# Three edits to a graph and expert kernel: POOL's rests, the order of ScalarE's scores and gate steps, and where the run counts are loaded

## The chip, the cores and the metric

One core of a Trainium2 chip. The metric is the device time of one execution in microseconds; the median of three runs before the change is 4437.22 us.

## The reference, cut to what matters

```python
edge_index = jnp.stack([src, dst])                 # 100000 edges, sorted by dst, 3125 nodes, 256 features
xn = _layernorm(x)
x = x + _L0_gnn_ref(xn, edge_index, ...) + _L0_mix_ref(xn[None], ...)[0]   # GCN, linear attention
x = x + _L0_ffn_ref(_layernorm(x)[None], ...)[0]   # graph attention gates four experts
xn = _layernorm(x)
x = x + _L1_gnn_ref(xn, edge_index, ...) + _L1_mix_ref(xn[None], ...)[0]
x = x + _L1_ffn_ref(_layernorm(x)[None], ...)[0]   # eight dense experts

# _L0_ffn_ref, the gated experts, with the graph attention that makes the gates (16 columns, 4 heads x 4 experts)
h = (x_flat @ W_gat).reshape(M, HEADS, NUM_EXPERTS)
e = leaky_relu((h * att_src).sum(-1)[src] + (h * att_dst).sum(-1)[dst], 0.2)
ee = exp(e - segment_max(e, dst)[dst])
agg = segment_sum(h[src] * (ee / segment_sum(ee, dst)[dst])[:, :, None], dst) + b_gat
scores = _layernorm(agg, ln_gamma, ln_beta).reshape(M, HEADS, NUM_EXPERTS).mean(1)
topk_s, topk_i = top_k(scores, 2); w = softmax(topk_s)
for ei in range(4):
    g = where(topk_i == ei, w, 0.0).sum(-1)
    out = out + g[..., None] * (gelu(x @ W1[ei] + b1[ei]) @ W2[ei] + b2[ei])
```

## The kernel before, in words

The nodes lie as 25 tiles (T) of 125 rows (P). The program is a sequence of blocks; in each block the five engines run their own instruction lists and meet at semaphores. The order on each engine is the order in which the code is written. `alone(eng, signal, value)` is a wait as an instruction of its own.

**The build of the adjacency (lines 436 to 625, about 50 to 632 us).** The counts of edges from each source to each destination are built as a dense matrix by one-hot matmuls. The destinations are split into 125 groups of 25 nodes (5 groups, TG, for each of 25 tiles). The edges are sorted by destination and cut into chunks of 128; a group works through its chunks in runs of four (RUN). There are 276 runs in all, 18 in the first group, two in most groups and one in many of the last. How many runs a group has, and how many came before, is data: `ranges_of` (L475) loads four numbers into an engine's registers.

- DVE makes, for each of a run's four chunks, the one-hot sources (`hot_src`, L519, three of the four) and the one-hot keys (`hot_key`, L522). Each of the four slots has one buffer, so it waits for `hot_used` of PE, one run back.
- ACT makes the fourth source in `make_sources` (L580, L584), one group ahead, and takes a finished group's counts out of PSUM in `take_out` (L593).
- PE loads the group's counts of runs (L475), multiplies two loop-block matmuls (L548, which start the sum) and then, per run and slot, one pair of matmuls (L557, 512 and 113 columns).
- POOL prepares the runs' keys (L496, L499), far ahead.

**The gated experts (lines 1990 to 2622, about 2100 to 2864 us).** PE runs four experts. Each has 5 groups of nodes (G); a group is eight pieces of the first layer (L2456, ACT's Gelu L2564) and five row tiles of the second (L2470, ACT's copy L2578). Experts 0 to 2 write rows to memory (SP, L2400), the last keeps them in `last_rows`.

Beside this the attention gates are made. The edges are in four blocks here (`earlier` is 1). For the first two, PE gathers the source rows by one-hot matmuls. For the last two, POOL gathers them with 256 indirect transfers (`gather_rows`, L2329), and after every second one it rests: two memsets of one column (`rest`, L2339), each awaited. DVE's `sum_up` waits for a block's gathers (`got`), forms the scores and, after ACT's two exponentials in `weigh` (L2548, L2549), the sums. ACT meets the `weigh` of each block at a fixed place of its list: that of the third block in the last group of expert 1, that of the fourth in group 1 of expert 2, after four pieces of that group.

When all sums are stored, POOL gathers them with 25 transfers (L2363). DVE forms the layer norm's variance, ACT its root (L2615), DVE the marks and their distance from the best, ACT the exponential (L2621), DVE the gates; PE turns them (`turn_gates`, L2531) and DVE adds the three stored experts' rows, weighted (L2294), then the last expert's (L2302), and takes the statistics of the next norm (L2307). SP loads the stored rows (L2443) when expert 2's are all stored and the sums are over (`sums_over`). ACT enters expert 3 only after `picks_over`, since `last_rows` holds the fourth block's gathered rows until then.

## Time and profile before

| | us |
|---|---|
| median of three runs (lowest, highest) | 4437.22 (4434.75, 4440.62) |
| profiled execution, its own time | 4442.14 |
| its span | 4440.2 |
| PE busy | 3688.1 (83%) |
| PE weight loads busy | 2662.1 (60%) |
| DVE busy | 2239.0 (50%) |
| ACT busy | 1345.7 (30%) |
| POOL busy | 720.6 (16%) |
| mean granted TensorE clock | 0.905 |

The profile is one execution, taken by the hardware's profiler. Busy time counts an engine's instructions, not its waits, register steps or the issue of transfers. The timeline lists instructions in order of time, merged where equal ones follow each other: start in us, duration in us, engine, line, operation, output<-inputs, count, and in brackets the idle time before it and what ended it ("issue": nothing that the profile shows; "remote": a signal from outside the engine's view). A "q" behind an engine's name is its sequencer.

### The profile page before, as it was taken

Reading aid. Unit: us, or ns where it says so; the run is one execution under the profiler, and the core shown is the slowest. Engines: PE = TensorE matmul, PEld = TensorE weight load, DVE = VectorE, ACT = ScalarE, POOL = GpSimd, SP = SyncE. Lnnn points to the kernel's source line nnn. Section 1 sums busy time; section 2 is a strip of 40 time slices with the busy share of each in tenths; the row PEclk is TensorE's granted clock in tenths of the full one; section 3 lists DMA queues with packets and bytes.
Section 4 is the critical chain, followed back from the end, with each engine's and each line's share of the span. In section 5 each row is a group of like instructions: output and inputs, shape, how many; then the busy total and the mean of one; then the engine's idle time right before and its main releaser. Section 6 shows DMA issues by size and latency. Waiting matters only on the chain. (4 is left out here: it accounts for less than half of the span.)

```text
span 4440.2 us, 92119 instructions
## 1 busy us (share of the span) xinstructions
PE 3688.1 (83%) x23892; PEld 2662.1 (60%) x23943; DVE 2239.0 (50%) x5781; ACT 1345.7 (30%) x2980; POOL 720.6 (16%) x1416
## 2 busy tenths in 40 slices
PE   4888867499969898996889627689798999799998
PEld 2444435366648757964777415479698544467766
DVE  6888877888840021125677330610402867533333
ACT  2555541477740010042111212410000144133333
POOL 3222210000000000001566632000001565000000
PEclk9999985688879989998999858889999999799999
DMA  3111230132234403501221211245154000100000
GB/s 110 44 71 75 84 120 0 57 95 85 66 111 160 151 5 146 202 22 18 76 63 32 40 45 57 91 148 190 62 186 166 1 1 1 21 14 14 7 14 29
DMA packets 124636, 319.63 MB, mean 72 GB/s; under 512 B 42658, under 2 KB 74897, under 8 KB 109228
## 3 DMA queue, kind: packets, MB, share of 16 engines
q1 hardware_dynamic: 111332, 302.42, 19.6%
q0 software_dynamic: 9760, 8.89, 1.4%
q10 hardware_dynamic: 3404, 6.53, 0.4%
q8 instruction: 78, 1.28, 0.1%
q14 instruction: 62, 0.51, 0.0%
HBM read 245.52 MB, written 72.43 MB: 72 GB/s over the span
## 5 line engine op out<-in xcount | busy, mean ns | idle before, releaser
L557 PE MATMUL ps<-hot_key,hot_src 128*126 128x512 bf16 (+1 forms) x2208 | 416.8, 314 | 38.5 <-DVE hot_key L522 21.0
L522 DVE TENSOR_SCALAR hot_key<-col_iota,run_keys 128x625 bf16<-128x625 int16 x1104 | 394.9, 380 | 0.0
L1338 PE MATMUL ps<-gnn_u_thirds,near 125*128 125x256 bf16 x3000 | 337.2, 275 | 23.3 <-issue 23.3
L557 PEld LDWEIGHTS ps<-hot_key,hot_src 128*126 128x126 bf16 x2208 | 212.5, 136 | 234.3 <-DVE hot_key L522 171.6
L1338 PEld LDWEIGHTS ps<-gnn_u_thirds,near 125*128 125x128 bf16 x3000 | 331.0, 141 | 27.8 <-issue 25.0
L2456 PE MATMUL ps<-xnT,ew 128*128 (+2 forms) x640 | 189.2, 449 | 158.3 <-ACT ehT L2564 123.7
L519 DVE TENSOR_SCALAR hot_src<-col_iota,run_srcs 128x125 bf16<-128x125 int16 x828 | 212.3, 256 | 97.0 <-PE ps L557 52.0
L2456 PEld LDWEIGHTS ps<-xnT,ew 128*128 128x128 f32 x640 | 123.1, 199 | 211.6 <-ACT ehT L2564 135.4
L866 PE MATMUL ps<-row_hot,slot_hot 128*128 128x512 f16 x1088 | 221.4, 357 | 2.3 <-DVE row_hot L1079 2.2
L3650 DVE SCALAR_TENSOR_TENSOR xres<-ps,shares,xres 125x256 f32 x200 | 96.8, 484 | 241.6 <-PE ps L3615 220.7
L2470 PE MATMUL ps<-ew,ehT 128*125 128x256 f32 x800 | 203.5, 398 | 0.0
L3604 PE MATMUL ps<-xnT,f 128*128 x640 | 185.4, 437 | 12.1 <-ACTq L3623 4.5
L1079 DVE TENSOR_SCALAR row_hot<-row_iota,row_of 128x670 f16<-128x670 int16 x544 | 190.5, 394 | 0.0
L1338 PE MATMUL ps<-agg_u_thirds,near 125*128 125x257 bf16 x1500 | 175.0, 277 | 10.2 <-issue 9.7
L3604 PE MATMUL ps<-f_h1T,f 128*128 128x313 f32 (+1 forms) x640 | 180.1, 434 | 0.0
L3615 PE MATMUL ps<-fo,f_h2T 128*125 128x256 f32 x800 | 179.2, 379 | 0.0
L1338 PEld LDWEIGHTS ps<-agg_u_thirds,near 125*128 125x128 bf16 x1500 | 169.4, 141 | 16.3 <-issue 15.3
L1338 PE MATMUL ps<-gcn_u_thirds,near 125*128 125x256 bf16 x1500 | 167.4, 275 | 12.5 <-DVEq L1557 12.5
L3631 ACT ACTIVATE f_h1T<-ps,norm_shift,norm_scale 128x313 f32<-128x313 f32 (+1 forms) x160 | 98.0, 612 | 261.5 <-PE ps L3604 261.5
L1620 POOL MEMSET block_mask<- 128x128 f32 x1 | 0.2, 204 | 1090.6 <-POOLq L1537 1090.6
L1338 PEld LDWEIGHTS ps<-gcn_u_thirds,near 125*128 125x128 bf16 x1500 | 165.3, 141 | 14.2 <-issue 12.9
L2500 PE MATMUL ps<-table_thirds,rows_room 125*128 125x144 bf16 x2304 | 154.8, 228 | 14.8 <-issue 9.2
(571 smaller groups left out, 6898.6 us busy)
## 6 DMA issues: line engine op xcount, KB each, us to landing
near<-adjacency SPq DMA_DIRECT2D x80, 1562.5 KB, 6.5
adjacency<-counts SPq DMA_DIRECT2D x125, 312.5 KB, 2.2
own_in<-own_rows SPq DMA_DIRECT2D x34, 512.0 KB, 4.1
expert_rows<-rows_y SPq DMA_DIRECT2D x75, 125.0 KB
rows_room<-expert_rows SPq DMA_DIRECT2D x25, 375.0 KB
pair_in<-high_rows SPq DMA_DIRECT2D x34, 256.0 KB, 4.8
pair_in<-low_rows SPq DMA_DIRECT2D x34, 256.0 KB, 5.7
rows_room<-key_rows SPq DMA_DIRECT2D x8, 1024.0 KB
```

Source lines behind the costliest of these rows:

```text
L519: nc.vector.tensor_scalar(hot_src[:, j, 0:P], col_iota[:, 0:P], run_srcs[:, ds(at, 1), j:j + 1].rearrange("p a j -> p (a j)"), None, ALU.i ...
L522: nc.vector.tensor_scalar(hot_key[:, j, :], col_iota[:], run_keys[:, ds(at, 1), j:j + 1].rearrange("p a j -> p (a j)"), None, ALU.is_equal ...
L557: last = nc.tensor.matmul(sums[:, b:e], hot_src[:, j, :], hot_key[:, j, b:e], start=False, stop=True, skip_group_check=True)
L866: last = nc.tensor.matmul(ps[:, bank, 0:e - b], slot_hot[:, c % RING, :], row_hot[:, c % RING, b:e], start=False, stop=True, skip_group_ch ...
L1079: nc.vector.tensor_scalar(row_hot[:, c % RING, :], row_iota[:], row_of[i][:, c:c + 1], None, ALU.is_equal).then_inc(routes_made, 1)
L1338: last = nc.tensor.matmul(ps[:, j, 0:width], lead_tiles[BUF[j]][:, k, :], parts.thirds[:, k, i, :], start=(k == 0 and i == 0), stop=(k == ...
L2456: last = nc.tensor.matmul(ps[:, piece % 2, 0:n], w1[i][:, c, m * 128:(m + 1) * 128], xnT[:, c, ds(g * NG + first, n)], start=(c == 0), sto ...
L2470: last = nc.tensor.matmul(o, hT[:, c, j * P:(j + 1) * P], w2[i][:, c, :], start=False, stop=(c == 3))
L2500: last = nc.tensor.matmul(pick_bank(piece % 2, k, many)[:, slot * MIDS * HROW:(slot + 1) * MIDS * HROW], src_hot[piece % 2][0:P, tier, edg ...
L3604: last = nc.tensor.matmul(ps[:, piece % 2, 0:n], (w1, w2)[stage][i][:, c, m * 128:(m + 1) * 128], moving, start=(c == 0), stop=(c == 1))
L3615: last = nc.tensor.matmul(o, h2T[:, c, j * P:(j + 1) * P], wo[i][:, c, :], start=(c == 0), stop=(c == 1))
L3631: nc.scalar.activation(hT[:, m, first:first + n], ps[:, piece % 2, 0:n], ACT.Relu, scale=norm_scale[:, stage, ds(e, 1), m], bias=norm_shif ...
```

## The change

It has three parts, and one that goes with the third.

1. POOL: the rest after every second gather is one awaited memset, not two.
2. ACT: the `weigh` of the fourth block stands in group 4 of expert 2, no longer in group 1; the root of the variances and the exponential of the odds stand in group 3 of expert 3, ahead of its rows 0 and 3 (before: in group 2 ahead of row 0, and between groups 2 and 3). On PE `turn_gates` stands in group 4 of expert 3, no longer in group 3.
3. PE in the build: the run counts of the next group are loaded behind the first pair of matmuls of every run, and no longer between two groups; only the first group of a tile still loads ahead of its runs.
4. ACT in the build: `make_sources` returns the count that `take_out` needs, so a group takes one load of the counts, not two.

```diff
@@ the build, PE
                     with pe.Fori(0, T) as tile:
+                        _, runs, before, _ = ranges_of(mybir.EngineType.PE, tile * TG)
                         for k in range(TG):
                             group = tile * TG + k
-                            _, runs, before, _ = ranges_of(mybir.EngineType.PE, group)
...
                                     last.then_inc(hot_used, 1)
+                                    if j == 0 and k < TG - 1:
+                                        _, next_runs, next_before, _ = ranges_of(mybir.EngineType.PE, group + 1)
+                            runs, before = next_runs, next_before
@@ the build, ACT
-                        first, runs, before, upto = ranges_of(mybir.EngineType.Activation, group)
+                        first, runs, before, _ = ranges_of(mybir.EngineType.Activation, group)
...
-                        return upto
+                        return before
...
-                            make_sources(tile * TG + k + 1)
-                            _, _, _, upto = ranges_of(mybir.EngineType.Activation, tile * TG + k)
-                            take_out(tile, k, upto)
+                            take_out(tile, k, make_sources(tile * TG + k + 1))
@@ the gated experts, POOL
                                 if j % 2:
-                                    rest(b * (SLOTS // 2) + (j // 2 - SLOTS))
-
-                        def rest(n):
-
-                            for k in range(2):
-                                nc.gpsimd.memset(idle[:], 0.0).then_inc(rested, 1)
-                                alone(pool, rested, n * 2 + (k + 1))
+                                    nc.gpsimd.memset(idle[:], 0.0).then_inc(rested, 1)
+                                    alone(pool, rested, b * (SLOTS // 2) + (j // 2 + 1 - SLOTS))
@@ the gated experts, PE
-                        expert(3, 1, 0, 3)
-                        expert(3, 1, 3, 4, ahead_of_rows=turn_gates)
-                        expert(3, 1, 4, G)
+                        expert(3, 1, 0, 4)
+                        expert(3, 1, 4, G, ahead_of_rows=turn_gates)
@@ the gated experts, ACT
-                        expert(2, 0, 1)
-                        expert(2, 1, 2, after_piece=weigh_within(earlier * 2 + 1))
-                        expert(2, 2, G)
-
-                        def root_of_variance(rows):
+                        expert(2, 0, 4)
+                        expert(2, 4, G, after_piece=weigh_within(earlier * 2 + 1))
+
+                        def gate_steps(rows):
                             if rows == 0:
                                 act.wait_ge(var_ready, 1)
                                 nc.scalar.activation(gstd, gvar, ACT.Sqrt).then_inc(std_ready, 1)
+                            if rows == 3:
+                                act.wait_ge(marks_ready, 1)
+                                nc.scalar.activation(odds, odds, ACT.Exp).then_inc(odds_ready, 1)
 
                         act.wait_ge(picks_over, 1)
-                        expert(3, 0, 2)
-                        expert(3, 2, 3, after_row=root_of_variance)
-                        act.wait_ge(marks_ready, 1)
-                        nc.scalar.activation(odds, odds, ACT.Exp).then_inc(odds_ready, 1)
-                        expert(3, 3, G)
+                        expert(3, 0, 3)
+                        expert(3, 3, 4, after_row=gate_steps)
+                        expert(3, 4, G)
```

How the instructions move. On PE, in the build's second group of a tile, the difference is this (+ in the changed kernel; L475 is the load of the run counts, L557 the hot matmuls, L551 the end of the loop over runs, L545 and L548 the next group's wait and loop-block matmuls):

```order
 L557 MATMUL ps<-hot_key,hot_src 126x512
 L557 MATMUL ps<-hot_key,hot_src 126x113
+L475 ISA
+L475 TENSOR_LOAD ranges_row
 L553 REGISTER_ALU
 L557 MATMUL ps<-hot_key,hot_src 126x512
...
 L551 REGISTER_ALU
 L551 COMPARE_AND_BRANCH
-L475 ISA
-L475 TENSOR_LOAD ranges_row
 L545 REGISTER_ALU
 L548 ISA
```

The load has gone from the place between the loop's end and the next group into the loop's body, where every run meets it.

On ACT, in expert 2, before (L2564 Gelu of the pieces, L2548 and L2549 the exponentials of `weigh`, L2578 the copies of the rows; the loop that follows is groups 2 to 4, then comes expert 3):

```order
L2559 UNCONDITIONAL_BRANCH
L2564 ACTIVATE ehT<-ps,eb 128x313 x4
L170 ISA
L2548 ACT_TABLE_LOAD
L2548 ACTIVATE rows_room<-rows_room 128x512
L2549 ACTIVATE rows_room<-rows_room 128x512
L2564 ACT_TABLE_LOAD
L2564 ACTIVATE ehT<-ps,eb 128x312 x4
L2578 ACTIVATE rows_y<-ps 125x256 x5
L2559 REGISTER_ALU
L2559 COMPARE_AND_BRANCH
```

and in the changed kernel, ahead of these the loop over groups 0 to 3, behind them that over groups 0 to 2 of expert 3 (L2558 is the Gelu, L2542 and L2543 `weigh`, L2572 the copies):

```order
L2553 UNCONDITIONAL_BRANCH
L2558 ACTIVATE ehT<-ps,eb 128x313 x4
L170 ISA
L2542 ACT_TABLE_LOAD
L2542 ACTIVATE rows_room<-rows_room 128x512
L2543 ACTIVATE rows_room<-rows_room 128x512
L2558 ACT_TABLE_LOAD
L2558 ACTIVATE ehT<-ps,eb 128x312 x4
L2572 ACTIVATE rows_y<-ps 125x256 x5
L2553 REGISTER_ALU
L2553 COMPARE_AND_BRANCH
```

The steps are the same; three whole groups of expert 2 have gone from behind them to ahead of them.

## Rows read from the trace of the kernel before

**Rows 1.** Waits of the gated experts, 2105 to 2860 us: who waited, for whom, us, times, longest

```profile
PE ps L2456 <- ACT ehT L2564: 123.7, 10, 108.2
ACT L2548 <- DVEq L2160: 105.3, 1, 105.3
DVE last_rows L2258 <- ACT last_rows L2615: 88.2, 1, 88.2
...
DVE rows_room L2144 <- DMA last_rows<-node_table,src_idx: 51.3, 1, 51.3
...
ACT rows_y L2578 <- remote: 16.4, 2, 8.2
```

**Rows 2.** Timeline of the build: a two-run group, then two one-run groups

```profile
304.44 3.16 PE L557 MATMUL ps<-hot_key,hot_src 128*126 128x512 bf16 x16
...
305.23 0.26 DVE L519 TENSOR_SCALAR hot_src<-col_iota,run_srcs 128x125 bf16<-128x125 int16 x1 [0.71 <-POOL run_keys L496]
...
308.13 0.48 PE L548 MATMUL ps<-loop_blocks,own_ident 125*126 x2 [0.54 <-issue]
...
308.66 0.70 PE L557 MATMUL ps<-hot_key,hot_src 128*126 128x512 bf16 x3
...
586.20 1.30 PE L557 MATMUL ps<-hot_key,hot_src 128*126 128x512 bf16 x8
...
588.12 1.30 PE L557 MATMUL ps<-hot_key,hot_src 128*126 128x512 bf16 x8
```

**Rows 3.** Waits of DVE in the build, 60 to 632 us

```profile
DVE hot_src L519 <- PE ps L557: 52.0, 74, 1.1
DVE hot_src L519 <- POOL run_keys L496: 35.1, 50, 0.7
```

**Rows 4.** Timeline of POOL: one rest and the next gather

```profile
2136.44 0.12 POOL L2339 MEMSET att_idle<- 128x1 f32 x1
2136.72 0.10 POOL L2339 MEMSET att_idle<- 128x1 f32 x1 [0.15 <-issue]
2137.67 0.99 POOL L2329 DMA_INDIRECT rows_room<-node_table,src_idx  x1 [0.85 <-issue]
```

**Rows 5.** Line 2339: engine, count, ns min/median/max, first and last start

```profile
L2339 POOL MEMSET att_idle<- x256: 98/112/384, 2136.4 to 2617.7; 128x1 f32 x128
```

**Rows 6.** Timeline of ACT in experts 2 and 3: first pieces of groups, and `weigh`

```profile
2501.62 0.52 ACT L2564 ACTIVATE ehT<-ps,eb 128x313 f32<-128x313 f32 x1 [1.78 <-PE ps L2456]
...
2521.83 0.52 ACT L2564 ACTIVATE ehT<-ps,eb 128x313 f32<-128x313 f32 x1 [0.67 <-PE ps L2456]
...
2630.78 1.28 ACT L2548 ACT_TABLE_LOAD   x1 [105.27 <-DVEq L2160]
...
2654.22 0.52 ACT L2564 ACTIVATE ehT<-ps,eb 128x313 f32<-128x313 f32 x1 [0.67 <-PE ps L2456]
...
2739.03 0.52 ACT L2564 ACTIVATE ehT<-ps,eb 128x313 f32<-128x313 f32 x1 [0.67 <-PE ps L2456]
```

**Rows 7.** Line 2363, the gathers of the sums, columns as above

```profile
L2363 POOL DMA_INDIRECT sums_got<-edge_sums,end_i x25: 992/997/1042, 2662.5 to 2693.8; - x25
```

**Rows 8.** Timeline of DVE: last asking, variances, gates, last statistics

```profile
2655.87 0.15 DVE L2060 TENSOR_SCALAR block_f<-block_f 128x1 f32<-128x1 f32 x1
...
2701.74 0.18 DVE L2255 TENSOR_SCALAR last_rows<-last_rows 128x25 f32<-128x25 f32 x1
...
2812.81 0.34 DVE L2287 COPY gates<-ps 125x100 f32<-125x100 f32 x1 [8.33 <-PE ps L2531]
...
2861.79 1.73 DVE L2307 BATCH_NORM_STATS2 norm_stats<-xres 125x6 f32<-125x256 f32 x5
```

**Rows 9.** Timeline of SP: the loads of the stored experts' rows

```profile
2741.57 63.79 SPq L2443 DMA_DIRECT2D rows_room<-expert_rows  x25
```

**Rows 10.** Lines 475 and 551 on PE's sequencer: count, ns min/median/max, first and last start

```profile
L475 PEldq TENSOR_LOAD <-ranges_row x125: 327/334/544, 46.4 to 628.7; - x125
...
L551 PEldq COMPARE_BRANCH  x276: 67/207/239, 61.6 to 630.5; - x138
```

More of the change, by code:

```diff
@@ L600, in _ @@
                         for k in range(TG):
-                            make_sources(tile * TG + k + 1)
-                            _, _, _, upto = ranges_of(mybir.EngineType.Activation, tile * TG + k)
-                            take_out(tile, k, upto)
-                    for k in range(TG):
-                        if k < TG - 1:
-                            make_sources((T - 1) * TG + k + 1)
-                        _, _, _, upto = ranges_of(mybir.EngineType.Activation, (T - 1) * TG + k)
-                        take_out(T - 1, k, upto)
+                            take_out(tile, k, make_sources(tile * TG + k + 1))
+                    for k in range(TG - 1):
+                        take_out(T - 1, k, make_sources((T - 1) * TG + k + 1))
+                    _, _, _, all_runs = ranges_of(mybir.EngineType.Activation, OWNERS - 1)
+                    take_out(T - 1, TG - 1, all_runs)
                     act.wait_ge(deg_ready, 1)
```

## The prediction

> **What bounds the kernel now.** The page gives TensorE (PE) as busy for 83% of the span, but that is an average over stages with different limits, so I read each edit in its own stage. I began with the list of waits of the attention stage (2105 to 2860 us), where two of the three edits lie. Its longest single waits are one event [rows 1]: ScalarE (ACT) sits 105.3 us in front of `weigh` until VectorE (DVE) has the scores of the last block, and PE sits 108.2 us for ACT's Gelu, because that `weigh` stands in the middle of ACT's loop over expert 2. DVE in turn waits 51.3 us for the gathers that POOL issues. So from 2525 us on only POOL's pace counts; behind it stand 3.5 groups of expert 2 and all of expert 3, of which PE could have done a good part in the hole. The 88.2 us that DVE waits at L2258 for ACT's root are the same thing seen later: the variances are ready and ACT has not got there.
>
> The third edit lies in the build of the adjacency (50 to 632 us). There I read the timeline of PE and DVE and the sequencer's records of two lines. One group of 25 nodes with two runs takes 4.22 us from its first hot matmul to the next group's (304.44 to 308.66), with 0.54 us of pure issue before the loop-block matmuls [rows 2]. DVE, which makes the one-hot operands, waits 52.0 + 35.1 = 87.1 us in the stage [rows 3]; these are the only idle microseconds there that a faster PE can win, and about 10 of them belong to the start.
>
> **Edit 1, one memset per rest (POOL).** A pair of gathers with its rest takes 3.5 us. The second memset starts 0.28 us after the first and ends 0.26 us after it; the 0.85 us from the awaited memset to the next gather stand behind whichever is last, so they stay [rows 4]. There are 256 memsets, most near 0.11 us and some up to 0.38 [rows 5]; 128 go, at 0.26 each: 33 us. DVE waits 51.3 us for POOL's last gather [rows 1], more than that, so all of it arrives at the exponentials: their start, R, moves from 2630.8 [rows 6] to 2597.6. Bounds: 0, if the transfers and not the issue limited the gathers, and 38, if the memsets that go were mostly the longer ones. Against 0 speak the 25 gathers of the sums, issued with no rest at 1.3 us each [rows 7], faster than the new pace.
>
> **Edit 2, `weigh` and the gate steps later in ACT's order.** A group of an expert takes 20.2 us (2501.62 to 2521.83) [rows 6]. Now ACT meets `weigh` in group 1 of expert 2, at 2525.5. In the new order the rest of group 1, groups 2 and 3 and half of group 4 run first: 3 x 20.2 = 60.6 more, so ACT and PE arrive at 2586 and wait about 11 us for R = 2597.6. Before, these stood between R and the copy of the gates (R + 182.0 [rows 6, 8]): half a group and 3 groups of expert 2, then groups 0, 1, 2 of expert 3 and the eight pieces of group 3. Now there stand: the other half of group 4 of expert 2 (23.4, as 2630.8 to 2654.2 [rows 6]), a wait of about 2 for `picks_over` (DVE is through with its asking at R + 25.2 [rows 8]), four groups of expert 3 (80.8), the eight pieces of the last one (9 with a table load), some 4 for the tables of the root and the exponential, and 24 that the 25 gathers of the sums cost. That cost is seen before: the three groups left of expert 2 take 84.8 us (2654.22 to 2739.03 [rows 6]) instead of 60.6, and ACT waits twice 8.2 us for signals from elsewhere [rows 1] exactly while POOL issues those gathers (2662.5 to 2693.8 [rows 7]). I leave this price in on both sides. Sum: 23.4 + 2 + 80.8 + 9 + 4 + 24 = 143, against 182: 39 us, of which I keep 38.
>
> What is late next is DVE: its part behind the gates (50.7 us, 2812.81 to 2863.5 [rows 8]) doesn't shrink, and since the gates are now turned one group later, PE gains some 20 us more than arrive. The variances are ready at R + 71 [rows 8] and the root is asked for near R + 119, so the gathers have 48 us to spare. SP's 25 loads of expert rows (63.8 us [rows 9]) no longer wait for expert 2 but for `sums_over`, near R + 32, and end near R + 96, before the gates at R + 143; without that cover their whole length would count. Bounds of this edit: 14, if the dense gathers hurt twice as much beside these loads, and 49, if ACT's waits at the dense gathers shrink by half or so because expert 3 stores nothing.
>
> **Edit 3, the run counts loaded inside the runs.** On PE the load and its address step leave the gap between groups (100 of 125 boundaries; each tile's first group still loads in the open) and go behind the first of a run's four pairs, in every run. The load alone has a median of 334 ns [rows 10], with its register steps 0.55 us. For a two-run group, with S its first hot matmul: the second pair comes at S + 0.67 (0.31 before), the fourth at S + 1.22. The sequencer needs 1.1 us for a run's register steps and its branch (the branch alone 0.21 [rows 10]; an estimate), 1.68 with the load, so the second run starts at S + 1.68. DVE starts on the operands after next when PE has used the first pair, at S + 0.80 as before (305.23), and takes 3.50 for eight, the period less its idle 0.71 [rows 2]. Second run: second pair S + 2.35, fourth S + 2.89, the loop-block matmuls 0.28 later and the next S another 0.53 later, 3.70 against 4.22. Gain 0.52; DVE would be free at S + 4.30 and is started at S + 4.50, so it still isn't the bound. In a one-run group (586.20 to 588.12, 1.92 us [rows 2]) the sequencer had run ahead of the array and the load was covered; now its fourth pair ends later, 2.03, a loss of 0.1. Of the 100 boundaries 82 end a group of two or more runs, 18 one of a single run: 82 x 0.52 - 18 x 0.1 = 41 us. In long groups a run stays at DVE's 1.75 us, half of 3.50, since 1.68 still fits below it. ACT loses one of its two loads per group and is not waited for. Bounds: 77 won (DVE's 87 less the start), and 83 lost, if the 151 additional loads were all exposed (151 x 0.55). I take 41, nearest to the row of the issue gap, 0.54 x 82 = 44.
>
> [...]
>
> **Sum.** 33 + 38 + 41 = 112 us. From the profiled execution's own 4442.1 us (span 4440.2) this gives 4330. That execution is 4.9 above the median of the runs, 4437.2; from the median it is 4325, my forecast.
>
> **Rivals.**
> [...]
> - The load in the run isn't covered. With the longest load on PE, 544 ns [rows 10], the second pair comes at S + 0.88, the second run at S + 1.89, its fourth pair at S + 3.31 and the next S at 4.12: 0.10 x 82 won, 0.3 x 18 lost, together 3 us. 4437 - 71 - 3 = 4363. Against it: the median of 334.
> - Slower: the shorter rest starves the other engines. While the 25 gathers go out without rests, ACT and PE lose 24 us in some 33, 0.73 per us; in the stretch with two memsets a group takes 20.2 us, no more than elsewhere, so two suffice. If one memset did not, the loss would run over the 450 us of resting gathers. The gains and the 11 us of slack before R cover 123 us, so it decides from 0.27 us per us, a third of the dense price; at half the dense price 164 are lost: 4437 - 112 - 11 + 164 = 4478. Against it: the awaited memset and the 0.85 us behind it stay, and they are most of the rest.
> - The edits do nothing, because some other wait is behind each: 4437.
>
> **Chances.** Forecast, with its own spread 4295 to 4345: 0.62. Attention part smaller: 0.15. Load not covered: 0.14. Starvation: 0.06. Nothing: 0.03. A range of 4290 to 4395 takes in the first three cases and most of the bounds. A measurement of this kernel can tell about 0.2%, 9 us, from no change: faster 0.92, within 0.02, slower 0.06.
>
> **What would show it.** In the changed profile: 128 memsets, pair pitch 3.25 us; ACT's wait at `weigh` 5 to 20 us instead of 105, and PE's with it; DVE's wait for the root about 50; from the gates to the end of the norm's statistics still 51; build groups of two runs at 3.7 us with no issue gap before the loop-block matmuls, one-run groups at 2.0, DVE's idle there near 46. Pair pitch at 3.5, two-run groups at 4.1 or more, ACT's wait at `weigh` above 40, or expert groups over 21 us while POOL gathers at rest pace would each prove a step wrong.

## The result, and the profile after

| | before | changed |
|---|---|---|
| median of 4 runs, us | 4438.92 (4434.75 to 4442.48) | 4340.61 (4337.22 to 4343.19) |
| profiled execution, us (span) | 4442.14 (4440.2) | 4337.22 (4335.5) |
| mean granted TensorE clock | 0.905 | 0.914 |

The ratio is 0.9778, with a 95% interval of 0.9766 to 0.9791: the change saves 98.3 us. The forecast was 4325 (4290 to 4395), that is 112 us. Cut by stage, the span shrank by 104.7 us: the build by 23.1 (41 forecast), the stage from the first gather to the end of the norm's statistics by 74 (71 forecast), everything else by 7.6. So the attention stage came as forecast, and the build gave little more than half.

**The attention stage.** The list of waits (2105 to 2770 us; who waited, for whom, us, times, longest), against [rows 1]:

```profile
PE ps L2451 <- ACT ehT L2558: 56.6, 9, 22.9
...
DVE last_rows L2258 <- ACT last_rows L2608: 46.7, 1, 46.7
...
ACT L2542 <- DVEq L2160: 20.0, 1, 20.0
...
ACT last_rows L2572 <- remote: 17.6, 2, 10.9
```

ACT's wait at `weigh` fell from 105.3 to 20.0 us, PE's longest wait for ACT from 108.2 to 22.9, and DVE waits 46.7 us for ACT's root instead of 88.2. The waits for a "remote" signal are still there; they return below.

POOL, one rest and the pair behind it, and the line of the memset (count, ns min/median/max, first and last start), against [rows 4] and [rows 5]:

```profile
2109.01 1.00 POOL L2329 DMA_INDIRECT rows_room<-node_table,src_idx  x1 [0.30 <-issue]
2110.01 0.11 POOL L2334 MEMSET att_idle<- 128x1 f32 x1
2110.98 1.00 POOL L2329 DMA_INDIRECT rows_room<-node_table,src_idx  x1 [0.85 <-issue]
2112.28 1.00 POOL L2329 DMA_INDIRECT rows_room<-node_table,src_idx  x1 [0.30 <-issue]
2113.27 0.12 POOL L2334 MEMSET att_idle<- 128x1 f32 x1
```

```profile
L2334 POOL MEMSET att_idle<- x128: 113/113/318, 2110.0 to 2559.5; 128x1 f32 x128
```

The 0.85 us behind the awaited memset stayed, and the pair takes 2113.27 - 2110.01 = 3.26 us. ACT and DVE, the places of [rows 6] and [rows 8], in their timelines:

```profile
2508.52 0.52 ACT L2558 ACTIVATE ehT<-ps,eb 128x313 f32<-128x313 f32 x1 [0.67 <-issue]
...
2528.74 0.52 ACT L2558 ACTIVATE ehT<-ps,eb 128x313 f32<-128x313 f32 x1 [0.67 <-PE ps L2451]
...
2572.65 1.28 ACT L2542 ACT_TABLE_LOAD   x1 [20.02 <-DVEq L2160]
...
2690.90 1.28 ACT L2608 ACT_TABLE_LOAD   x1
```

```profile
2712.46 0.34 DVE L2287 COPY gates<-ps 125x100 f32<-125x100 f32 x1 [8.47 <-PE ps L2526]
...
2761.43 1.73 DVE L2307 BATCH_NORM_STATS2 norm_stats<-xres 125x6 f32<-125x256 f32 x5
```

The gathers of the sums and SP's loads, the places of [rows 7] and [rows 9]:

```profile
L2358 POOL DMA_INDIRECT sums_got<-edge_sums,end_i x25: 996/1000/1045, 2603.7 to 2635.0; - x25
```

```profile
2602.92 64.42 SPq L2438 DMA_DIRECT2D rows_room<-expert_rows  x25
```

SP's loads are issued by 2667.3, 45 us ahead of the gates. A group still takes 20.2 us (2528.74 - 2508.52) beside the resting gathers. R is 2572.65; the gates are copied 139.8 us later (182.0 before), and from there to the last statistics it is 50.7 us as before.

**The build.** A slow and a fast two-run group on PE, against [rows 2]; DVE's waits from 60 to 609 us and its line 519 in the same window, against [rows 3]; and line 475 on PE's sequencer, against [rows 10]:

```profile
360.94 0.47 PE L548 MATMUL ps<-loop_blocks,own_ident 125*126 x2
361.48 0.47 PE L557 MATMUL ps<-hot_key,hot_src 128*126 128x512 bf16 x2
362.48 2.64 PE L557 MATMUL ps<-hot_key,hot_src 128*126 128x512 bf16 x14 [0.53 <-DVE hot_key L522]
364.99 0.48 PE L548 MATMUL ps<-loop_blocks,own_ident 125*126 x2
365.52 0.47 PE L557 MATMUL ps<-hot_key,hot_src 128*126 128x512 bf16 x2
366.16 1.47 PE L557 MATMUL ps<-hot_key,hot_src 128*126 128x512 bf16 x8 [0.16 <-DVE hot_key L522]
367.81 1.03 PE L557 MATMUL ps<-hot_key,hot_src 128*126 128x512 bf16 x6 [0.18 <-DVE hot_key L522]
368.68 0.46 PE L548 MATMUL ps<-loop_blocks,own_ident 125*126 x2
```

```profile
DVE hot_src L519 <- PE ps L557: 30.2, 62, 1.6
DVE hot_src L519 <- POOL run_srcs L499: 7.3, 7, 1.1
DVE hot_src L519 <- issue: 5.3, 27, 0.2
DVE hot_src L519 <- POOL run_keys L496: 0.7, 1, 0.7
```

```profile
L519 DVE TENSOR_SCALAR hot_src<-col_iota,run_srcs 128x125 bf16<-128x125 int16 x826 | 212.0, 257 | 58.4 <-PE ps L557 30.2 <-POOL run_srcs L499 7.3 <-issue 5.3
```

```profile
L475 PEldq TENSOR_LOAD <-ranges_row x252: 327/333/729, 45.8 to 604.9; - x126
```

The gap of pure issue before the loop-block matmuls is gone. The second group takes 3.69 us (364.99 to 368.68), the forecast 3.70; the first takes 4.05, and the difference stands in front of its second pair, which starts 1.00 us after the first instead of 0.64. The median of PE's loads hardly moved (334 to 333 ns), but 69 of the 252 now take over 400 ns; before, 3 of 125 did. The profile names DVE (hot_key L522) as the releaser of that second pair; what stands in front of it in PE's own queue is the load, from 361.6 to 362.3 as shown further down.

The list of DVE's waits sums to 43.5 us, close to the 46 that the prediction named as a sign, and yet the build fell 18 us short. That list leaves out every wait of 0.15 us or less. With them DVE is idle for 58.4 us ahead of L519 (the figure behind the second bar), 29 less than the 87.4 of the kernel before, where nearly all of the idle time stood in longer waits. The sign looked fulfilled and wasn't.

From PE's records, the groups' periods summed by kind (start of a group's loop-block matmuls to the next group's; a "last" group is the fifth of a tile, with the next load in the open):

```
groups            count   before    after   change   forecast
one run              18     37.1     39.4     +2.3       +1.8
two runs             65    273.2    248.4    -24.8      -33.8
three and more       17    160.5    157.8     -2.7       -8.8
last of a tile       25    110.1    113.0     +2.9        0
```

Split by whether the load in the group's first run took over 400 ns, two-run groups have a median of 3.70 us with a fast load (33 of them) and 3.93 with a slow one (32); one-run groups 2.02 and 2.31; three-run groups 5.57 and 5.83, against 5.96 before. (For one of the 18 one-run groups the trace has no load between its start and the next group's; it is in neither class.) So the question for the experiments was what makes a load slow; beside it, whether the parts add up, and what the rests between gathers really guard.

### The profile page after: what moved, and what is told of

The parts are those of the page before. It is cut to its first block and busy times, and to the rows that moved or that the text cites. A ratio compares the mean times of both kernels' runs of the same rounds, so it can differ in the third digit from the quotient of the medians.

```text
span 4335.5 us, 91902 instructions
## 1 busy us (share of the span) xinstructions
PE 3669.1 (85%) x23942; PEld 2659.2 (61%) x23943; DVE 2243.8 (52%) x5781; ACT 1344.7 (31%) x2979; POOL 699.8 (16%) x1288
## 5 line engine op out<-in xcount | busy, mean ns | idle before, releaser
L557 PE MATMUL ps<-hot_key,hot_src 128*126 128x512 bf16 (+1 forms) x2208 | 414.5, 314 | 75.5 <-DVE hot_key L522 48.1
L522 DVE TENSOR_SCALAR hot_key<-col_iota,run_keys 128x625 bf16<-128x625 int16 x1104 | 394.6, 379 | 0.0
L557 PEld LDWEIGHTS ps<-hot_key,hot_src 128*126 128x126 bf16 x2208 | 216.0, 137 | 264.6 <-DVE hot_key L522 182.9
L519 DVE TENSOR_SCALAR hot_src<-col_iota,run_srcs 128x125 bf16<-128x125 int16 x828 | 212.5, 257 | 68.4 <-PE ps L557 30.2
L3609 PEld LDWEIGHTS ps<-fo,f_h2T 128*125 128x125 f32 x800 | 150.2, 188 | 26.2
```

The lines of the kernel that those rows point to most:

```text
L519: nc.vector.tensor_scalar(hot_src[:, j, 0:P], col_iota[:, 0:P], run_srcs[:, ds(at, 1), j:j + 1].rearrange("p a j -> p (a j)"), None, ALU.i ...
L522: nc.vector.tensor_scalar(hot_key[:, j, :], col_iota[:], run_keys[:, ds(at, 1), j:j + 1].rearrange("p a j -> p (a j)"), None, ALU.is_equal ...
L557: last = nc.tensor.matmul(sums[:, b:e], hot_src[:, j, :], hot_key[:, j, b:e], start=False, stop=True, skip_group_check=True)
L3609: last = nc.tensor.matmul(o, h2T[:, c, j * P:(j + 1) * P], wo[i][:, c, :], start=(c == 0), stop=(c == 1))
```

## The experiments

In the expectations S is the start of a group's loop-block matmuls, 0.54 us ahead of the first hot matmul, which is the prediction's S. Twelve kernels ran in three sets of four, each set on one chip beside the kernel before: 4437.7 us on the first, 4416.6 on the second, 4439.6 on the third. Differences below are to the kernel before, or the changed kernel, of the same set; in the second set, where the changed kernel didn't run, ratios are compared.

### First set: the edits apart

`e1`: the kernel before with one memset per rest (the POOL hunk of the diff alone). 

> The kernel before with edit 1 alone (one memset per rest; ACT's order and the build as before). Theory: only POOL's pace counts before R, so the exponentials of the last block start 32 us earlier in the stage and everything behind them keeps its length (R to the copy of the gates 182 us): 4437 - 32 = 4405, pair pitch 3.27 us. Rival: the gain of edit 1 needs edit 2, because ACT's late order gives part of it back behind R: under 20 us, 4420 or more.

`e2`: the kernel before with the two hunks on `expert(...)` and `gate_steps` alone. 

> The kernel before with edit 2 alone (weigh in group 4 of expert 2, gate steps in group 3 of expert 3, gates turned in group 4). In the changed kernel ACT still waited 20 us at weigh; with the old rests R is 32 us later against ACT's arrival, so the wait is 52 us, and R to the copy of the gates is 140 us instead of 182: 4437 - 42 = 4395. Rival: the shorter stretch behind R came partly from edit 1 (transfers of the last block out of the way); then R to gates stays above 150 and the kernel above 4405.

Measured: `e1` 4406.85 us (ratio 0.9935, 0.992 to 0.995), -30.8; `e2` 4397.61 (0.9915, 0.990 to 0.993), -40.1. ACT's wait at `weigh` in each (timeline of `e1`, then of `e2`):

```profile
2599.56 1.28 ACT L2544 ACT_TABLE_LOAD   x1 [72.37 <-DVEq L2160]
```

```profile
2628.39 1.28 ACT L2547 ACT_TABLE_LOAD   x1 [39.99 <-DVEq L2160]
```

The first theory holds for both edits, each works without the other: R to the gates is 177.3 us in `e1` (2599.56 to 2776.87; 182 forecast) and 141.0 in `e2` (2628.39 to 2769.40; 140 forecast). The wait in `e2` was forecast at 52 and is 40: ACT came to `weigh` 12 us later than I had worked out from the changed kernel (at 2588.4, close to the 2586 of the prediction), which cost nothing, since R waits for POOL.

`e3`: the kernel before with both halves of edit 3. 

> The kernel before with edit 3 alone (the run counts loaded inside the runs on PE, ACT one load per group less). The build ended 23 us earlier in the changed kernel, and the three edits lie in stages apart: 4437 - 23 = 4414, build groups of two runs 3.7 to 3.8 us. Rival: the edits interact by the DMA or by where the code lies, and the sum of the three alone differs from 98 us by more than 10.

`e3pe`: PE's half only. 

> As the last one, but only PE's half of edit 3: ACT keeps its two loads per group (250 instead of 126). Theory A, register loads of different engines delay one another: in the changed kernel 69 of PE's 252 loads took over 400 ns, so with twice as many loads on ACT some 80 to 110 do, and the gain falls to 15 to 20 us (4417 to 4422). Theory B, PE's loads in a run are slow for a reason of PE's own and ACT is never waited for: as many slow loads and the same time as with both halves, 4414.

Measured: `e3` 4412.7 us (0.9939, 0.9925 to 0.9952), -25.0; `e3pe` 4405.7 (0.9932, 0.9919 to 0.9946), -32.0; these two can't be told apart. The three edits alone sum to 30.8 + 40.1 + 25.0 = 95.9, together they gave 98.3: they add up. The loads of `e3pe`:

```profile
L475 PEldq TENSOR_LOAD <-ranges_row x252: 327/332/627, 45.6 to 599.2; - x126
L475 ACTq TENSOR_LOAD <-ranges_row x250: 303/307/632, 49.7 to 603.2; - x125
```

Both theories fell. With twice as many loads on ACT, not more but fewer of PE's were slow: 20 of 252, against 70 in `e3`. PE's instructions are the same in both, so neither the number of loads on ACT nor PE's own code decides. What moved is ACT's take-out of a group, and with it the moment at which SP issues the group's store. I therefore set every register load of PE, ACT and POOL against the time since SP's last issue of a store (`adjacency <- counts`). All loads that started 0.7 to 1.2 us behind it were slow (over 400 ns), in the kernel before, the changed one, `e3` and `e3pe` alike: 10 of 10, 43 of 43, 40 of 40, 20 of 20. In the pair of groups above SP issued at 360.84 and at 365.10:

```profile
360.84 0.33 SPq L618 DMA_DIRECT2D adjacency<-counts  x1
```

```profile
365.10 0.33 SPq L618 DMA_DIRECT2D adjacency<-counts  x1
```

```profile
L475 POOLq TENSOR_LOAD <-ranges_row x1: 555/555/555, 361.5 to 361.5; - x1
...
L475 PEldq TENSOR_LOAD <-ranges_row x1: 687/687/687, 361.6 to 361.6; - x1
```

```profile
L475 POOLq TENSOR_LOAD <-ranges_row x1: 317/317/317, 365.3 to 365.3; - x1
...
L475 PEldq TENSOR_LOAD <-ranges_row x1: 342/342/342, 365.7 to 365.7; - x1
```

(The last two fences are line 475 in 0.3 us of each group.) The loads 0.64 and 0.76 us behind the issue take 555 and 687 ns, those 0.16 and 0.56 us behind it 317 and 342.

`e3pe` shows a second thing. With 50 fewer slow loads its 65 two-run groups are together no shorter than those of `e3` (248.2 and 247.9 us). The 17 of them that open a tile take 3.95 us (median), against 3.74 in `e3`: behind each of the 17 the loop-block matmuls start 0.14 us after the end of ACT's take-out, which the trace names as their releaser, and in `e3` they don't wait for it. So ACT "is not waited for" holds only with ACT's second load gone, and part 4 of the change is needed, by some 17 x 0.21 = 3.6 us (an estimate from these medians).

### Second set: moving the load, moving the store, and the gathers of the sums

`j2`, in the build on PE:

```
-                                    if j == 0 and k < TG - 1:
+                                    if j == 2 and k < TG - 1:
```

> The changed kernel with PE's load of the run counts behind a run's third pair instead of its first. In the runs so far every register load that starts 0.75 to 1.25 us after SP issued a group's store took 450 to 730 ns, on PE, ACT and POOL alike, and nearly none outside; PE's first-run loads start at S + 0.67, inside that window. Theory A, SP's store delays register loads: behind the third pair the load starts at about S + 1.2, past the window, so under 20 of 252 loads take over 400 ns (69 before), groups of two runs come to 3.7 us, and the kernel gains 5 to 12 us on the changed one (4340.6): 4329 to 4336. Theory B, the load is slow in a group's first run because PE meets that code there first: 60 to 70 loads stay slow, and the time stays within 3 us of 4341.

Measured: 4334.4 us, ratio 0.9819 (0.9805 to 0.9833), against 0.9778 and 0.9788 for the two measurements of the changed kernel: worse by some 15 us, although only 37 loads were slow. The build ended at 619.8 us, that of `space` (below), which has the changed kernel's build and ran on the same chip, at 605.2. That the time lies in theory A's range of 4329 to 4336 is luck: the range was worked out from another chip, on which the kernel before took 21 us more. Theory A's count missed too (37 slow loads, under 20 forecast); it is right on what makes a load slow and wrong on what that is worth. DVE's waits in its build say why:

```profile
DVE hot_src L519 <- PE ps L557: 73.8, 145, 1.3
```

In the changed kernel the load sits behind pair 1, and the pairs behind it follow closely. Behind pair 3 it delays the fourth pair of each run, the last of the group too: by the medians over the 65 two-run groups the last two pairs start at S + 2.85 and 3.54 and the next group at 3.99; in the changed kernel, at 3.19, 3.47 and 3.77. The place behind the first pair is the better of the two tried.

`splate`, on SP:

```
                             alone(sp, group_out, tile * TG + (k + TG + 1))
+                            for _ in range(24):
+                                sp.sem_inc(waits_met, 1)
```

> The changed kernel with SP issuing each group's store about 1 us later (24 semaphore increments between its wait and the store; nothing else is moved). Theory A, SP's store delays register loads: PE's first-run loads now start before the store does and are fast, and those loads that happen to lie 0.75 to 1.25 us behind the new issue are slow instead, whoever makes them; of PE's 252 under 35 take over 400 ns. Theory B, PE's own code is the cause: the same 69 loads stay slow. The time moves by under 10 us either way, since the store is waited for by nobody for four groups.

Measured: 4316.2 us, ratio 0.9774 (0.9758 to 0.9789), no different from the changed kernel's 0.9778; the build ended at 601.6, 3.6 us before that of `space`. The store went out some 1.4 us later, and of the 124 loads in a group's first run 5 were slow instead of 68. But 65 of 252 were slow all the same: now those of the second run, and more of ACT's (37) and POOL's (26). The number forecast (under 35) missed; that the slow loads follow the store is shown, since nothing but SP's issue was moved. Here 79 of 79 loads in the window were slow.

`space`, on POOL, and `spgate`, which has `space` and this order besides:

```
                                                     bounds_check=LIST2 - 1, oob_is_err=False).then_inc(ends_got, 16)
+                            if d % 2:
+                                nc.gpsimd.memset(idle[:], 0.0).then_inc(rested, 1)
+                                alone(pool, rested, earlier * SLOTS + (d // 2 + 1))
```

```
-                        expert(3, 1, 0, 4)
-                        expert(3, 1, 4, G, ahead_of_rows=turn_gates)
+                        expert(3, 1, 0, 3)
+                        expert(3, 1, 3, 4, ahead_of_rows=turn_gates)
+                        expert(3, 1, 4, G)
...
-                        expert(3, 0, 3)
-                        expert(3, 3, 4, after_row=gate_steps)
-                        expert(3, 4, G)
+                        expert(3, 0, 2)
+                        expert(3, 2, 3, after_row=gate_steps)
+                        expert(3, 3, G)
```

> The changed kernel with the same rest (one awaited memset per pair) also between the 25 gathers of the sums. Theory A, POOL's dense issue of gathers holds up signals of the other engines: ACT's two long waits for signals from elsewhere (10.9 us the longest) go, the groups of experts 2 and 3 beside those gathers take 20.2 us instead of 26.5 and 42.8, R to the copy of the gates shrinks from 140 to about 118, and the kernel gains 20 to 23 us: 4318 to 4321. The gathers end 8 us later, which nobody waits for. Theory B, the cost comes from what the gathers and SP's loads of rows move through the DMA engines, whatever their spacing: the waits stay, and the time is 4341.

> The last kernel, and the gate steps and the turning of the gates one group earlier (group 2 and group 3 of expert 3), since ACT waited 20 us at weigh, where 11 were forecast. If the gathers' spacing gives its 22 us, the root is asked for near R + 76, 3 us ahead of the variances (R + 79), the gates are copied near R + 100, DVE's 51 us behind them stay, and ACT's last rows are there before DVE comes to them: another 15 to 20 us, 4299 to 4305. Rival: DVE or the gates' inputs are late (ACT waits over 10 us for the variances, or DVE for SP's rows, which land up to R + 92), and the gain over the last kernel is under 8 us.

Measured: `space` 4314.6 us, ratio 0.9779 (0.9764 to 0.9795), so no gain over the changed kernel's ratio; `spgate` 4295.8, 0.9726 (0.971 to 0.9741), 18.8 us below `space` (15 to 20 forecast). The trace of `space` has the 119 us from R to the gates that theory A wanted, but so have `j2` and `splate`, whose gathers of the sums are as dense as ever. ACT's waits in `j2` beside them (2623 to 2660 us), all short and none remote:

```profile
ACT last_rows L2572 <- PE ps L2465: 19.6, 10, 2.7
ACT ehT L2558 <- PE ps L2451: 7.0, 13, 0.6
```

In this set's four traces the 20 us weren't lost at all, and the kernel before took 21 us less than on the first chip. This set could say nothing on the spacing.

### Third set: a control, the combination, and no rests

> The changed kernel once more, beside the next three on one chip, because the last four kernels ran on a chip where the kernel before took 4416.6 us instead of 4437.7, and there none of them showed the 20 us that ACT lost beside the 25 gathers of the sums, with or without rests between these. Theory A, the loss belongs to that chip's or that stretch's conditions and not to the kernel: where before takes about 4438 the loss is there (R to the copy of the gates 140 us), where before takes about 4417 it isn't (119 us), and the ratio to before is 0.978 on both. Theory B, it is the new order that loses or keeps it: the ratio differs between the chips by over 0.003.

`gate` is `spgate` without the rests of `space`. 

> The changed kernel with the gate steps and the turning of the gates one group earlier (group 2 and group 3 of expert 3), the 25 gathers of the sums dense as in the changed kernel. The move gave 16 us in the traces of the last two kernels (R to gates 119 to 100). Without the loss of 20 us on this chip: the same as with spaced gathers, 18 to 20 us under the changed kernel of this call. With the loss: the root is asked for later, R to gates about 120, and again some 20 us under the changed kernel; the spacing of the gathers is then decided by the next kernel, which has it.

`best` is `spgate` with 9 of the 24 semaphore increments of `splate`. 

> The changed kernel with the gate steps and gates one group earlier, the rests between the gathers of the sums, and SP's store of a group issued about 0.5 us later (9 semaphore increments). Theory: SP's issue moves from S + 0.0 to about S + 0.4 to 0.7, so the window in which register loads are slow lies at S + 1.2 to 1.9, between PE's first-run load (S + 0.7) and the second one (S + 2.3): under 30 of PE's 252 loads take over 400 ns, groups of two runs come to 3.70 to 3.75 us, and the build ends 6 to 10 us before that of the changed kernel. Together 24 to 32 us under the changed kernel of this call. Rival: the store comes late for the take-out four groups on, or other loads fall into the window, and the build gains under 3 us.

Measured, with the kernel before at 4439.6:

| kernel | us | ratio (95%) | build ends | R to gates |
|---|---|---|---|---|
| `again` | 4343.0 | 0.9788 (0.9772 to 0.9805) | 606.1 | 139.8 |
| `gate` | 4322.4 | 0.9737 (0.9720 to 0.9753) | 606.5 | 119.8 |
| `best` | 4288.7 | 0.9659 (0.9643 to 0.9676) | 594.9 | 98.7 |

Here the loss is there. `again` agrees with its theory A as far as it goes, a chip with the kernel before near 4438 and R to the gates 140 us; what the changed kernel takes on a chip of the other kind wasn't run. `gate` and `best` tell the cause apart. ACT's waits beside the gathers of the sums, in `gate` (2607 to 2650 us) and in `best` (2594 to 2637 us):

```profile
ACT last_rows L2573 <- remote: 18.3, 2, 9.5
ACT last_rows L2573 <- PE ps L2465: 9.8, 2, 7.2
```

```profile
ACT last_rows L2578 <- PE ps L2470: 13.4, 7, 2.7
ACT ehT L2564 <- PE ps L2456: 7.5, 13, 1.1
```

What ACT waits for there isn't outside the core. The timeline of `gate` has PE's last row tile and ACT's last two copies:

```profile
2620.76 1.99 PE L2465 MATMUL ps<-ew,ehT 128*125 128x256 f32 x8
...
2633.19 0.38 ACT L2573 ACTIVATE last_rows<-ps 125x256 f32 x1 [8.80 <-remote]
...
2643.09 0.38 ACT L2573 ACTIVATE last_rows<-ps 125x256 f32 x1 [9.52 <-remote]
```

```profile
2562.62 1.28 ACT L2548 ACT_TABLE_LOAD   x1 [10.93 <-DVEq L2162]
...
2639.74 1.28 ACT L2614 ACT_TABLE_LOAD   x1
2644.72 0.22 ACT L2614 ACTIVATE last_rows<-last_rows 128x25 f32<-128x25 f32 x1 [3.70 <-DVEq L2258]
```

And the store issued half a microsecond later (0.54) gave the build 11.2 us. PE's loads in `best`: 13 of 252 over 400 ns; 60 of the 65 two-run groups have a fast load, with a median of 3.69 us.

```profile
L475 PEldq TENSOR_LOAD <-ranges_row x252: 328/332/612, 45.4 to 591.8; - x126
```

`best` beats the changed kernel by 54.4 us and the kernel before by 151. Its parts, 20.0 + 21.1 + 11.2 = 52.3, leave 2 to the scatter. The forecast of 24 to 32 missed: it had the step of the gates and 6 to 10 us for the build, and nothing for the lost 21 us that the rests bring back.

`rest0` is the changed kernel without `if j % 2:` and the two lines under it. 

> The changed kernel with no rest at all between the gathers of the edges. Theory A (the rests guard the other engines): without them POOL issues a pair in 2.6 us, and for over 300 us ACT and PE lose time beside it as they did beside the 25 dense gathers, 0.3 to 0.7 us per us: experts' groups of 27 us and more, 4400 or above. Theory B (the rests only cost): the gathers end up to 85 us earlier, of which the 20 to 25 us count that ACT waits at weigh, since ACT's own work bounds the stage from there: 20 us under the changed kernel of this call, groups of 20.2 us as before.

Measured: 4623.3 us, ratio 1.0416 (1.0399 to 1.0434), 280 us above `again`. Theory A holds, at a far higher price than the 4400 it named. The gathers' pairs go out in 2.6 us, and yet the last of the 256 starts 635 us after the first, not 449. The windows of `rest0`, then of `again` (stretch, length, busy us and instructions of PE, PE's weight loads, DVE, ACT and POOL, granted clock, DMA share, GB/s):

```profile
2110.00:2240.00 130.00, 40.55 (x126) 24.25 (x124) 7.69 (x22) 7.10 (x16) 99.88 (x100) 0.63 0.21 42
```

```profile
2110.00:2240.00 130.00, 126.75 (x1365) 109.69 (x1364) 84.75 (x163) 17.98 (x39) 85.32 (x116) 1.00 0.29 80
```

While POOL issues without a rest, PE is busy for 41 of 130 us instead of 127, a loss of 0.66 us per us, and its granted clock is 0.63 (1.00 in `again`). ACT and DVE wait 112 and 165 us at a stretch for PE's late signals, of which the one that ends DVE's wait stands 48.8 us behind its matmul (2241.93 to 2290.73) (waits of `rest0`, 2105 to 2770 us):

```profile
DVE gat_chosen L2105 <- remote: 217.9, 3, 164.9
...
ACT ehT L2555 <- remote: 165.1, 7, 111.8
```

In this kernel the rests are no idle padding: one memset per pair is enough, and no rest at all costs 280 us.

## Why the prediction was right, and where it was not

**Edit 1** was right: 33 us forecast; R in the stage moved 31.7 us in the trace, and the edit alone gave 30.8. Taking the memset's price from the timeline of one rest (0.26) and not from its duration (0.11) was the point: 128 x 0.11 would have said 14.

**Edit 2** was right in its size: R to the gates 143 forecast, 139.8 measured; ACT's wait at `weigh` "about 11", measured 20.0, at the upper end of the 5 to 20 that it allowed; 38 us kept, 40.1 measured alone and 42 in the trace. Why ACT came earlier than worked out is open: its wait is 13.8 us in `gate` and 16.8 in `again`, which are the changed kernel up to R, on another chip. DVE's 50.7 us behind the gates stood to 0.1, and SP's loads were hidden. The text saw that the gates are now turned a group later and PE gains 20 us "more than arrive"; what it left unsaid is that this was a choice of the change, worth 20 us, and that DVE's wait for the root, 46.7 us in the changed kernel, left room for the other one. The 24 us left in on both sides were near the 20 to 21 that they turned out to be where they occur: in the result and on two of the three chips of the experiments, and on one not at all. The prediction took them for a fixed price of the gathers.

**Edit 3** was mis-sized: 41 us forecast, 23.1 in the trace, 25.0 alone. The steps of its working:

- The two-run group at 3.70 us with a load of 334 ns: a median of 3.70 in the groups with a fast load. The mechanism and its arithmetic hold.
- "The load alone has a median of 334 ns": that median was taken for every load. The change moved the first-run loads to 0.13 us behind the first hot matmul, and in about half of the groups SP issues a store some 0.6 to 0.8 us ahead of that; 68 of the 123 loads in a group's first run were slow, the last groups of the tiles included. The row with 544 as its maximum showed that slow loads exist; I put them into a rival as if chance made them, when they have a cause and a place that the change moves into. This is the term of the sum that was mis-sized. That costs 32 x 0.23 = 7.4 us in two-run groups, most of the 9.0 missing there, and 10 x 0.29 + 8 x 0.26 = 5 in those of one and three runs.
- "ACT loses one of its two loads per group and is not waited for": right for the kernel as changed; `e3pe` shows that with both loads it is waited for in 17 groups.
- One-run groups: 2.03 forecast, 2.02 with a fast load. Right.
- Three and more runs: 0.52 a group forecast, 0.16 measured, 6.1 us short over 17 groups. Eight of the ten of three runs had a slow load; with a fast one (two groups) such a group gains 0.39, so part of the miss here is not the store's and stays open.
- The last groups of a tile, costed at nothing, lost 2.9 us. Their next load, still in the open, stands 4.0 us behind the group's start, and 14 of 24 of these now fell into the store's window.

`best` is the check on this reading: with the store moved and nothing in the build's code on PE touched, 11.2 of the missing 17.9 us came.

The rival built on the slow load, 4363, was closer in kind than its chance of 0.14 said: it had the right mechanism for half of the loads in a group's first run (68 of 123 over 400 ns, where the median of all 252 is 333).

**Starvation** was the rival on the other side, with a third of the dense price as its point of decision. Its mechanism showed in `rest0`, without rests (0.66 us per us, 0.73 estimated), and with one awaited memset per pair none of it does: groups beside the resting gathers stayed at 20.2 us.

In the traces the build fell 18 us short, while the attention stage gave 3 us more than forecast and the stages that no edit touches 7.6: 104.7 us of 112. The medians show 98.3 instead of 104.7, because the profiled executions lie 3.2 us above (before) and 3.4 us below (changed) their medians. The median came 15.6 us above the forecast, inside the range. The attention stage came by the mechanism forecast, and so did the build, at little more than half its size.

## What to carry to other kernels

Before a register load is moved, look at what DMA is issued in the microsecond before its new place; a median over its old places was no price for the new one here (334 ns; in the new place 68 of the 123 loads in a group's first run took over 400). The stage in which POOL issues 256 gathers was kept open by short rests; how short they may be elsewhere is to be measured, since the price had a step here (nothing at one memset, 280 us at none). After a long wait has been removed, the waits that are left tell how far the next steps can be moved: DVE's 46.7 us for the root said that the gate steps could come earlier, and one step gave 20. And a list that leaves out short waits can make an engine look busier than it is.

## What the runs showed of the hardware

- Other engines' register loads were slow in a fixed window behind SP's issue of a store. Over the builds of the kernel before, the changed one and the twelve experiments (7157 loads of PE, ACT and POOL at line 475), 713 of 713 that started 0.60 to 1.25 us behind SP's issue took over 400 ns (418 to 737), 208 of 464 at 0.55 to 0.60 or 1.25 to 1.35 us, and 42 of 5980 elsewhere: the first load of each of the three engines in each kernel, made ahead of any store. The stores land 2.2 us after their issue (median of the 125 of the kernel before). What in the store does it wasn't tried.
- Beside dense indirect gathers on POOL (one per 1.3 us) signals between other engines came late: PE's to ACT stood 20.0 us behind its matmul in `again`, one to DVE 48.8 us in `rest0`, where DVE waited 165 us at a stretch. With one memset that POOL awaits per pair of gathers this doesn't show (0.02 us in `best`). Beside 25 such gathers the loss is some 20 us on the first and third chips, and none in the traces of the second. That would account for the 21 us by which the kernel before is faster there, but it wasn't profiled on that chip, so this is not shown. What distinguishes the chip is open, and so is whether the changed kernel itself would show a ratio other than 0.978 on it, since it didn't run there.
